# Softmax attention: scores of two heads in full precision side by side, output projected head by head, two transpose banks

## What is computed

```
def attn_a(x, Wq, Wk, Wv, Wo, bo):          # 16 heads of 64
    q, k, v = split_heads(x @ Wq), split_heads(x @ Wk), split_heads(x @ Wv)
    scores = q @ k.T * 64 ** -0.5 + slope[h] * (i - j)
    scores = where(i >= j, scores, -1e30)
    out = softmax(scores) @ v               # per head
    return merge_heads(out) @ Wo + bo
x = x + attn_a(layernorm(x), ...)
```

## Time and profile before

| | us |
|---|---|
| median of 3 runs | 6437.15 |
| lowest and highest | 6435.8, 6438.96 |
| the profiled execution's own time | 6438.86 |
| its span | 6437.1 |
| of it: start of the first pair to the end of the last (`stage_attn_a` without its head) | 53 to 2643 |
| one round of the pair loop, as 1357.75 to 1519.45 | 161.7 |
| first pair's start to the last one's end over 16, the change of batch in it | 161.9 |
| PE, DVE, ACT busy over the span | 66%, 72%, 71% |

### The profile page before, as it was taken

The page is one execution under the profiler, slowest core; times in us unless marked ns, Lnnn a source line. Parts: engine busy times, 40 slices in busy tenths (PEclk is TensorE's granted clock), DMA queues, the critical chain, the costliest instruction groups (busy, mean ns, idle before and its releaser), DMA issues. The chain is left out here.

```text
span 6437.1 us, 72186 instructions
## 1 busy us (share of the span) xinstructions
PE 4277.6 (66%) x23556; PEld 2298.1 (36%) x23556; DVE 4624.8 (72%) x6664; ACT 4576.2 (71%) x3663; POOL 1422.3 (22%) x1212
## 2 busy tenths in 40 slices
PE   6999999989999999744444444444544545444446
PEld 4666666666666666521011110110310111101104
DVE  5555555555555555559989898986599898989865
ACT  3555545545545555327999999999289999999992
POOL 0000000000000000004444444442044444444420
PEclk9999999999999999866777676766767666767767
DMA  1000000000000000017888988887288888888871
GB/s 37 6 6 6 6 6 6 6 6 6 6 6 6 6 6 2 3 74 160 180 183 184 188 175 187 185 181 161 101 165 180 182 183 188 175 187 185 180 159 56
DMA packets 154048, 632.56 MB, mean 98 GB/s; under 512 B 44934, under 2 KB 83016, under 8 KB 83528
## 3 DMA queue, kind: packets, MB, share of 16 engines
q0 software_dynamic: 73728, 536.90, 41.6%
q1 hardware_dynamic: 79944, 90.74, 4.2%
HBM read 69.50 MB, written 21.23 MB: 14 GB/s over the span
## 5 line engine op out<-in xcount | busy, mean ns | idle before, releaser
L1203 DVE SCALAR_TENSOR_TENSOR b_tiles<-b_ra_rep,b_cap,psum 128x1024 f32<-128x1024 f32 x1024 | 1261.0, 1271 | 247.7 <-PE psum L1434 236.0
L1434 PE MATMUL psum<-b_qT,b_kT 126*128 126x512 bf16 x2048 | 763.5, 483 | 501.2 <-DVE b_tiles L1203 498.4
L1447 PE MATMUL psum<-b_tiles,b_v_aug 128*32 128x512 f32 x2464 | 447.1, 810 | 679.7 <-ACT b_tiles L1347 679.7
L567 DVE CUSTOM_DVE_ANT_0 a_srow<-psum,a_bias 128x1024 f32<-128x1024 f32 (+7 forms) x768 | 679.4, 910 | 146.2 <-PE psum L703 73.8
L638 ACT ACTIVATE a_srow<-a_srow,a_nmax 128x640 f32<-128x640 f32 (+15 forms) x512 | 615.9, 1203 | 121.7 <-DVE a_nmax L573 90.9
L1210 DVE TENSOR_SCALAR b_tiles<-b_tiles 128x2048 f32<-128x2048 f32 x512 | 666.1, 1301 | 5.5
L199 POOL MEMSET ffn_rank<- 128x1 f32 x16 | 0.7, 99 | 2718.7 <-POOLq L74 2718.7
L1434 PEld LDWEIGHTS psum<-b_qT,b_kT 126*128 126x128 bf16 x2048 | 156.7, 108 | 1236.7 <-DVE b_tiles L1203 946.7
L1447 PE MATMUL psum<-X,b_v_aug 128*32 128x512 f32 x1632 | 294.8, 807 | 444.3 <-ACT X L1347 444.2
L1347 ACT ACTIVATE b_tiles<-b_tiles,b_sc 128x4096 f32<-128x4096 f32 x154 | 585.5, 3802 | 5.1
L725 PE MATMUL psum<-ident,a_srow 128*128 128x128 f32 x4352 | 577.7, 277 | 16.7 <-DVE a_pT L484 11.6
(11 more groups left out here) (219 smaller groups left out, 7321.0 us busy)
## 6 DMA issues: line engine op xcount, KB each, us to landing
b_tiles<-b_tiles POOLq DMA_DIRECT2D x308, 1024.0 KB, 12.1
X<-b_tiles POOLq DMA_DIRECT2D x204, 1024.0 KB, 13.1
b_ra_rep<-ra_scratch SPq DMA_DIRECT2D x32, 1024.0 KB, 6.7
a_wqk<-in_wqk_dram SPq DMA_DIRECT2D x64, 128.0 KB, 2.7
x_scratch<-X SPq DMA_DIRECT2D x8, 1024.0 KB, 10.6
kv_scratch<-b_tiles SPq DMA_DIRECT2D x4, 2048.0 KB, 8.5
X<-x_scratch SPq DMA_DIRECT2D x8, 1024.0 KB, 10.4
X<-in_x_dram SPq DMA_DIRECT2D x4, 1024.0 KB, 9.9
```

The costliest lines, as they stand in the source:

```text
L567: nc.vector.tensor_tensor_reduce(out=srow[:, row, a:z], in0=ps_scores(chunk0[u] + i, z - a), in1=bias[:, h, a:z], scale=1.0, scalar=-3e38, ...
L1203: nc.vector.scalar_tensor_tensor(out=a[:, s * HALF:(s + 1) * HALF], in0=ra_rep[:, j, s * HALF:(s + 1) * HALF], scalar=cap[:, j, k:k + 1], ...
L1434: last = nc.tensor.matmul(half_ps(s)[:, i * BANK:(i + 1) * BANK], kT[:, j, k * P:(k + 1) * P], qT[:, j, cs], start=True, stop=True)
L1447: last = nc.tensor.matmul(bank(4 + j)[32 * i:32 * i + 32, :], v_aug[:, j, k, :], y_slot(h, k)[:, i * BANK:(i + 1) * BANK], start=(k == 0), ...
```

## The change

The functions of `stage_attn_a` are rewritten; the other stages and the inputs stay.

- **Projections** go to `project(g, i)`: 8 banks for a pair instead of 16. One bank holds q (or k) of both heads, 64 rows each, in fp32 (`q_sb`, `k_sb`; ACT copies q with the scale in it, `copy_q`, DVE copies k). There is no rounded part and rest. They are issued in the last four steps of the pair before, one pair ahead; the last pair of a batch is a second copy of the body without them, and the first pair's stand ahead of the loop. V (`values`) is made in step 0, through the transpose banks.
- **Scores** (`scores(g, n, i)`): one step is a tile of both heads, longest tile first; a slot is 512 columns of both heads, in two banks: head 0 reads partitions 0 to 63 of q and k, head 1 partitions 64 to 127. They are fp32 matmuls, 64 rows deep. The mask is in the bias.
- **DVE's reductions** are 512 columns wide: 80 in a pair where there were 48. `nmax` of both heads is one `tensor_reduce`.
- **Transposes** (`transposes(g, n, i)`) go to two banks (4 and 5) in turn, two steps later; ACT copies the even blocks and DVE the odd ones. ACT's code of a step begins with both exponentials of the tile before.
- **Output**: the product with V is as it was; ACT copies it unscaled to `oT`, PE projects head by head (64 rows deep, banks 6 and 7), and DVE multiplies by the reciprocal sum as it adds on x (`scalar_tensor_tensor`, four of 256 columns for a pair of tiles). The transposes of the sums go.
- `order(n)` lays out a step for all engines: S are slots, V, T transposed blocks, A the product with V, O the output projection, P projections.

Worked out from `order`, the steps are: 0: S V S V S V S V; 1: S S S S; 2 and 3: S T T, four times; 4: S A T T S T T T S T T T; 5 the same with O for A; 6: S A T T S T T S T T; 7 with O; 8: S A T T T S T T T; 9 with O; 10: S A T T S T T; 11 with O; 12: S A T T T T; 13 with O; 14: S A T T; 15 with O; 16: A P T P T; 17: O P T P T; 18: A P P; 19: O P P. The T of step n are those of the tile of step n - 2.

```diff
+    tiles = list(reversed(range(TB)))
+    slots = [[(a, min(a + BANK, (it + 1) * P)) for a in range(0, (it + 1) * P, BANK)] for it in tiles]
+    slot0 = [sum(len(c) for c in slots[:n]) for n in range(TB + 1)]
+    NSL = slot0[TB]
+    NVE = 4
+    blocks = [[(h, a, min(a + 4, it + 1)) for h in range(2) for a in range(0, it + 1, 4)] for it in tiles]
+    evac0 = [NVE + sum(len(c) for c in blocks[:n]) for n in range(TB + 1)]
+    NEV = evac0[TB]
+    ROWS = 3
+    LAG = 2
+    STEPS = TB + 4
+    PROJ = ["q3", "k0", "k1", "k2", "k3", "q2", "q1", "q0"]
+    NPR = len(PROJ)
+    on_dve = [e % 2 == 1 for e in range(NEV)]
+    def count(upto):
+        return sum(on_dve[:upto])
+    n_dve = count(NEV)
     n_act = NEV - n_dve
-    av_step = {ib: 4 * (ib + 1) + LAG for ib in range(NIB)}
-    op_step = {ib: 4 * (ib + 1) + LAG + 2 for ib in range(NIB)}
-    STEPS = UNITS + LAG + 4
+    def order(n):
+        s = [("S", i) for i in range(len(slots[n]))] if n < TB else []
+        t = [("T", i) for i in range(len(blocks[n - LAG]))] if 0 <= n - LAG < TB else []
+        x = []
+        if n == 0:
+            x = [("V", i) for i in range(NVE)]
+        if n >= 4:
+            x = [("O", (n - 5) // 2) if n % 2 else ("A", (n - 4) // 2)]
+        if n >= TB:
+            x += [("P", 2 * (n - TB)), ("P", 2 * (n - TB) + 1)]
+        parts = max(len(s), len(x), 1)
+        seq = []
+        for i in range(parts):
+            seq += s[i:i + 1] + x[i:i + 1] + t[i * len(t) // parts:(i + 1) * len(t) // parts]
+        return seq
...
+        T_BANKS = (4, 5)
...
+            h, a, z = blocks[n][i]
+            il = tiles[n] % 2
+            if n % 2 == 0:
+                eng.wait_ge(av_done, g * NIB + n // 2)
+            copy(pT[:, h, a:z, il * P:(il + 1) * P], src[:, 0:(z - a) * P].rearrange("p (j i) -> p j i", i=P)
+                 ).then_inc(done, 1)
...
+            def body(b, hp, last):
+                g = b * PAIRS + hp
+                added = b * TB + TB + g * TB * 2
+                dve.wait_ge(bias_done, (g + 1) * 2)
+                for n in range(STEPS):
+                    for what, i in order(n):
+                        if what == "S":
+                            a, z = slots[n][i]
+                            c = slot0[n] + i
+                            if i == 0:
+                                dve.wait_ge(probT_done, g * NEV + (evac0[n - ROWS + 1] if n >= ROWS else 0))
+                            off = SEQ - P - tiles[n] * P
+                            for h in range(2):
+                                dve.wait_ge(scores_done, (g * NSL + c) * 2 + h + 1)
+                                dve.sem_inc(passed, 1)
+                                nc.vector.tensor_tensor_reduce(
+                                    out=srow[:, n % ROWS, h, a:z], in0=bank(c % 2 * 2 + h, 0, z - a),
+                                    in1=bias[:, h, off + a:off + z], scale=1.0, scalar=-3e38, op0=ALU.add, op1=ALU.max,
+                                    accum_out=cmax[:, n, h, i:i + 1]).then_inc(max_done, 1)
+                            if i + 1 == len(slots[n]):
+                                dve.wait_ge(max_done, (g * NSL + c + 1) * 2)
+                                nc.vector.tensor_reduce(nmax[:, n, :].unsqueeze(2), cmax[:, n, :, 0:i + 1], AX.X, ALU.max,
+                                                        negate=True).then_inc(nmax_done, 1)
+                        if what == "V":
+                            evacuate(dve, nc.vector.tensor_copy, g, None, i, True)
+                        if what == "T":
+                            evacuate(dve, nc.vector.tensor_copy, g, n - LAG, i, True)
+                        if what == "O":
+                            dve.wait_ge(op_done, g * NIB + i + 1)
+                            for m in (2 * i + 1, 2 * i):
+                                xt = env.X[:, bass.ds(b * TB + tiles[m], 1), :].rearrange("p a d -> p (a d)")
+                                il = tiles[m] % 2
+                                dve.wait_ge(zinv_done, g * TB + m + 1)
+                                for h in range(2):
+                                    dve.wait_ge(x_added, added + 4 * i + 2 * il + h)
+                                    dve.sem_inc(passed, 1)
+                                    nc.vector.scalar_tensor_tensor(out=xt, in0=bank(6 + h, il * D, (il + 1) * D),
+                                                                   scalar=zinv[:, m, h:h + 1], in1=xt, op0=ALU.mult,
+                                                                   op1=ALU.add).then_inc(x_added, 1)
+                        if what == "P" and not last and PROJ[i][0] == "k":
+                            blk = int(PROJ[i][1])
+                            dve.wait_ge(proj_done, (g + 1) * NPR + i + 1)
+                            nc.vector.tensor_copy(k_sb[:, blk * BANK:(blk + 1) * BANK], bank(i % 4)).then_inc(k_copied, 1)
+                    m = n - 1
+                    if 0 <= m < TB:
+                        dve.wait_ge(exp_done, (g * TB + m + 1) * 2)
+                        nc.vector.reciprocal(zinv[:, m, :], zsum[:, m, :]).then_inc(zinv_done, 1)
+                    if n == TB and not last:
+                        make_bias(g + 1, hp + 1)
...
+            def exponential(g, n, h):
+                width = (tiles[n] + 1) * P
+                act.wait_ge(nmax_done, g * TB + n + 1)
+                row = srow[:, n % ROWS, h, 0:width]
+                nc.scalar.activation(row, row, ACT.Exp, bias=nmax[:, n, h:h + 1],
+                                     accum_out=zsum[:, n, h:h + 1]).then_inc(exp_done, 1)
+            def body(b, hp, last):
+                g = b * PAIRS + hp
+                for n in range(STEPS):
+                    m = n - 1
+                    seq = order(n)
+                    if 0 <= m < TB:
+                        exponential(g, m, 0)
+                    for j, (what, i) in enumerate(seq):
+                        if j == min(1, len(seq) - 1) and 0 <= m < TB:
+                            exponential(g, m, 1)
+                        if what == "V":
+                            evacuate(act, copy, g, None, i, False)
+                        if what == "T":
+                            evacuate(act, copy, g, n - LAG, i, False)
+                        if what == "P" and not last and PROJ[i][0] == "q":
+                            copy_q(g + 1, i)
+                    if n >= 4 and n % 2 == 0:
+                        k = (n - 4) // 2
+                        act.wait_ge(av_done, g * NIB + k + 1)
+                        act.wait_ge(op_done, g * NIB + max(k - 1, 0))
+                        nc.scalar.activation(oT[:, k % 2, :], bank(6, 0, IB), ACT.Copy).then_inc(oT_done, 1)
...
+            def project(g, i):
+                w, blk = "qk".index(PROJ[i][0]), int(PROJ[i][1])
+                if i == 0:
+                    pe.wait_ge(wqk_loaded, (g + 1) * 32)
+                    pe.wait_ge(max_done, g * NSL * 2)
+                if i >= 4:
+                    if PROJ[i - 4][0] == "q":
+                        pe.wait_ge(q_copied, g * 4 + sum(p[0] == "q" for p in PROJ[:i - 3]))
+                    else:
+                        pe.wait_ge(k_copied, g * 4 + sum(p[0] == "k" for p in PROJ[:i - 3]))
+                for c in range(KC):
+                    last = nc.tensor.matmul(bank(i % 4), wqk_sb[:, w, c, :, :].rearrange("p a d -> p (a d)"),
+                                            xnT[:, c, blk * BANK:(blk + 1) * BANK], start=(c == 0), stop=(c == KC - 1))
+                last.then_inc(proj_done, 1)
...
+            def scores(g, n, i):
+                a, z = slots[n][i]
+                c = slot0[n] + i
+                if c == 0:
+                    pe.wait_ge(q_copied, (g + 1) * 4)
+                    pe.wait_ge(k_copied, (g + 1) * 4)
+                if c >= 2:
+                    pe.wait_ge(max_done, (g * NSL + c - 1) * 2)
+                pe.sem_inc(passed, 1)
+                for h in range(2):
+                    nc.tensor.matmul(bank(c % 2 * 2 + h, 0, z - a), q_sb[rows(h), tiles[n] * P:(tiles[n] + 1) * P],
+                                     k_sb[rows(h), a:z], start=True, stop=True, skip_group_check=True
+                                     ).then_inc(scores_done, 1)
+            def transposes(g, n, i):
+                h, a, z = blocks[n][i]
+                e = evac0[n] + i
+                if i == 0 or h != blocks[n][i - 1][0]:
+                    pe.wait_ge(exp_done, (g * TB + n) * 2 + h + 1)
+                evacuated(pe, g, e - 2)
+                for jt in range(a, z):
+                    last = nc.tensor.transpose(bank(T_BANKS[e % 2], (jt - a) * P, (jt - a + 1) * P),
+                                               srow[:, n % ROWS, h, jt * P:(jt + 1) * P], env.ident[:, :])
+                last.then_inc(probT_done, 1)
+            def product_with_v(b, g, k):
+                ib = NIB - 1 - k
+                pe.wait_ge(x_added, b * TB + TB + (g * NIB + k) * 4)
```

(36 more changed lines are left out.)

372 lines of the change are left out of this document (104 added, 268 removed).

## The result

The changed kernel takes 6503.8 us (median of 4 runs, 6498.6 to 6511.0) against 6437.7 (6435.8 to 6439.0) for the kernel before, run beside it: a ratio of 1.0103, with a 95% interval from 1.0091 to 1.0115. It is slower by 1%. The forecast was 6373, faster by 1%; 6503.8 lies inside the range that was given, but on the side that had 0.29.

What follows compares the result with a forecast made beforehand. PE was taken to bound the first attention: 132.0 us of work plus 24.6 of waits make a round 156.6 against 161.0, 70 us less over 16 rounds, +10 at batch ends, so 6373 us; range 6265 to 6550.

Steps and rivals of the forecast that it cites:

- the side that had 0.29: The whole kernel being slower after the change, chance 0.29, against faster 0.64 and same 0.07.
- the other case: Rival for the scores on PE: row halves do not overlap, +22 us a pair, about 6725 us, chance 0.11.
- the prediction's sign: Test on PE's score slots: the prediction would be wrong if a slot of both heads costs over 1.05 us.
- The other rule weighed: Partial overlap of the scores on PE: strict program order, slot 1.29 us, 6540 us; chance 0.10 shared with a 1.12 slot.
- the walk through the waits: PE's waits in one pair round, walked step by step through `order`: 5.9 + 13.5 + 2.7 + 2.5 = 24.6 us.
- Kind 2: Steps 4 to 15: a fourth or last block waits for DVE's copy behind reductions or additions, about 13.5 us.
- the tail: Short tiles at the end of a pair wait for each other, with P's between them: 2.7 us.
- O + 2.8: In steps with O, DVE's copy of the second block stands behind four additions, by O + 2.8 us.
- Kind 1: Steps 2 and 3: third block's bank waits for ACT's copy after both exponentials, 3.8 and 2.1 us, 5.9 in all.
- the loop's turn: Between pairs, while the engines turn the loop: 2.5 us of PE wait remain of 3.3.
- The ends of the batches: First projections stand alone and the last pair's short tiles are uncovered: +5 us each, +10 us.
- the waits are longer: Rival: PE waits 0.15 us more at each of 30 places, +4.5 us a pair, 6445 us; chance 0.15.

Runs made afterwards that it cites:

- s1_same_rows: Changed kernel with both heads' scores reading the same half of the rows (head 0's q and k, result wrong): 6908.9 us.
- a1_adds: Changed kernel with DVE adding head 0 on both tiles, then head 1 on both, so no addition waits for the one just before: 6396.6 us.
- d1_p_first: `a1_adds` with projections ahead of the product with V in steps 16 and 18 and of the output projection in step 19: 6341.2 us.
- a2_late: Changed kernel with DVE's additions of the O steps behind its first copy of the step instead of ahead of it: 6699.9 us.
- d4_all: `a1_adds` plus projections first in the tail, nine DVE copies given to ACT, second exponential later in steps 2 and 3: 6182.6 us.
- b1_two_banks: Kernel before with two transpose banks instead of three, DVE copying every second block instead of every third: 6816.8 us.
- a3_exp: Changed kernel with ACT's second exponential of a tile behind the step's first copy, in all steps: 6492.4 us.

## Why the prediction was wrong

**Right.** That PE bounds the stage and DVE and ACT do not by their sum. (DVE is busy for 91.3 us a round where some 95 was forecast; the terms listed for it add up to 99.) That two heads on two halves of the rows overlap fully: a slot is 0.86 + 0.20 and not 1.72, and `s1_same_rows` shows the price of the other case, 25 us a pair for 22 forecast. Taken at its word, the prediction's sign (a slot over 1.05) came true with 1.06, but 0.20 of that is the change of shape, which the sum had apart. By the speedup that the Trainium skill (TensorE: Matmul & The Clock Gate, "Measured speedup vs the span model") gives for four row tiles, a slot would have been 1.12 without the change of shape, an estimate; the trace disagrees, with 0.86, and 1.06 with the change of shape in it. The other rule weighed, that matmuls start and end in program order (the Trainium skill, TensorE: Matmul & The Clock Gate, Part 3), did not give a slot of three spans either: the first instructions of both heads start 6 ns apart in the trace (1768.016 and 1768.022), the second ones 7 ns apart (1768.549 and 1768.556), and the slot has two spans. That the change of shape costs 0.3 (0.34). That the third block waits for ACT in steps 2 and 3, and DVE's copies hold up the later steps. The stages behind are unchanged but for 3.4 us. PE's work of a round: 131.3 for 132.0.

**The step that failed is the walk through the waits, 24.6 for 32.6.** By its terms:

- *Kind 2, 13.5 for 15.9, and the tail, 2.7 for 7.7.* The walk took "O + 2.8" for the copy behind four additions, with additions bounded by the 0.422 of one multiplication. That holds for instructions that don't wait for each other: in `a1_adds` four take 1.58. Here each waits for the one just ahead, with 0.15 to 0.26 us between them: 2.41 for four. `a1_adds` removes that, and 7 us a round go, 1.4 of them the clock. In the profile before, DVE waits in this stage for its own instruction ahead only behind short ones (the parts of a maximum, a reciprocal), with under 0.04 us between them, so the duration was in the rows but this gap was not; the diff shows the dependence, `dve.wait_ge(x_added, ...)` ahead of each addition, and it should have been priced.
- *The tail, again.* Its tiles are short, and everything DVE does there is in PE's way: the bias of 2.46 us stands ahead of the additions in step 17, so that A of step 18 waits 2.31. The prediction named "P's between them" as cover, but P stands behind A in steps 16 and 18, and behind O in 19, not ahead of it. `d1_p_first` puts it ahead and the waits go.
- *The clock.* The sum had PE at one price throughout. Behind the 2.65 us wait the granted clock was 0.53, 1.4 us more in 13 of 14 rounds; in `a2_late`, with more idle time, it was 10 us a round, in `a1_adds` nothing in eight of fourteen rounds, in `d4_all` nothing in all fourteen.
- *Step 1 (1.4) and waits under 0.2 (2.8)* were taken at nothing. Step 1 has slots and no transposes, and two reductions of 0.61 each are longer than a slot of 1.06.
- *Kind 1 was too dear (5.9 for 3.9), the loop's turn too (2.5 for 0.9)*. For kind 1 the prediction's own figures, 6.8 us less the 4.1 at hand, give 2.7 a step, and not 3.8 and 2.1. At the turn nothing stands under "issue" any more: with projections at the end of the body PE has instructions to run while the engines turn, and what is left is the 0.78 that it waits for ACT's copy of q.
- *Luck in the rest.* These last four errors, +1.4 and +2.8 against -2.0 and -1.6, cancel to 0.6. So `a1_adds`, with the additions alone mended, has a round of 156.85 beside the forecast of 156.6; that agreement is partly luck.

**The ends of the batches** were +10 and came to +14, a small part of the miss. The sum had the projections at 14 us a batch, as PE's work, and +5 for a tail of short tiles. PE at the start of the first batch:

```profile
52.25 15.38 PE L696 MATMUL psum<-a_xnT,a_wqk 128*128 128x512 f32 x32 [1.61 <-ACT a_xnT L672]
68.41 1.13 PE L727 MATMUL psum<-a_k,a_q 64*128 64x512 f32 x4 [0.78 <-ACT a_q L636]
```

From the first projection to the first slot it is 16.2 us, 2.4 more than 13.8, with 0.78 of waiting for the last copy of q in it. In the second batch the same takes 17.0 (1392.11 to 1409.06), since the clock is low at first. No experiment tries these ends.

**Why a small error turned the sign.** A round was to gain 4.4 us, as the difference between 161.0 and a sum of 132.0 of work and 24.6 of waits, of which the second was an estimate of some thirty places. An error of a third in that term (8.0) is almost twice the gain. The rival "the waits are longer" was the right one, though not by 0.15 at thirty places: seven places had some 0.84 each and one of them the clock on top, 7.0 of the 8.0. And the prediction's own test was too wide: it would be wrong with more than 35 us of waits, while the gain was already gone at 29.0. Two banks for three, with DVE's larger share of the copies, were priced only as the waits of kind 1 and 2, 19.4 us; in the kernel before the same two alone are +23 us a round.

**What stays open.** How much of the small waits in `d4_all` a third transpose bank would take back was not tried: in the changed kernel the eight banks are all in use. How much of `b1_two_banks` is the bank and how much the division of the copies was not tried either. What decides where the clock falls is not shown, and so the 1.4 us a round, and the size of what `a2_late` and `a3_exp` lose by it, could not have been forecast from these rows. The cost of the projections that stand alone was only read from the starts of the pairs.

## What to carry to other kernels

Where a change trades work of the bounding engine against waits, the waits need as much care as the work: list every place, and ask whether the forecast margin is larger than their error. Price instructions in a row that wait for one another with the gap between them, and look first for another order of the two loops: here that was worth 107 us, more than the difference between the kernels. When an experiment misses, look whether the lost time is idle time or the same instructions at a lower clock. When a helper engine's chain is as long as the main engine's, moving its work within a step only moves the wait; give work to a third engine, or fill the wait with work that depends on neither.

## What the runs showed of the hardware

- Idle time of PE can cost twice. Stretches of 3 to 6.5 us at a granted clock of 0.53 to 0.57, near the 1.2 GHz level, began behind waits of 2.23 us (`d1_p_first`), 2.65 (the changed kernel) and 3.23 (`a2_late`). But the same 2.23 us (step 2) and 2.31 us (step 18) in the changed kernel and the same 2.65 us in `a3_exp` were followed by the full clock. What decides between them is not shown. Usual rounds with more idle time had more such stretches (none in `d4_all`, one in the changed kernel, five in `a2_late`), but `a3_exp`, with 2 us less of idle time than the changed kernel, had two or three in twelve of fourteen rounds. An edit elsewhere in the round moved them.
- fp32 matmuls of 64 rows on the two halves of the array run side by side at full speed: 1.06 us against 1.91 on the same half, for the same four instructions of 512 columns.
- A change of shape between 64 and 128 rows costs 0.34 us there and back (2.08 against 1.74 for a slot and two blocks), even where no data is waited for.
- An addition of DVE that waits by a semaphore for the one just ahead starts 0.15 us after its end on the same tile and 0.26 on the other; where it waits for the one two places ahead (`a1_adds`) there is no gap, and starts stand 0.39 apart.
